# Moving small products next to products of their tile shape in a fused attention and expert kernel

## The chip, the cores and the metric
The kernel runs on one core of a Trainium2 chip. The metric is the device time of one execution in microseconds (us). Before the change it is 894.55 us, the median of three runs (894.02 to 895.84). The engines are TensorE (PE, its weight loads are PEld), VectorE (DVE), ScalarE (ACT), GpSimd (POOL) and SyncE (SP), which issues most DMAs.

## What is computed
The input x has 16 batches of 512 rows of 256 values. Cut to what matters:

```python
xn = layernorm(x)
q = (xn @ Wq.T + bq) * 0.25              # 16 heads of 16
k, v = split(xn @ Wkv.T + bkv)           # one k and one v of 16, shared by all heads
p = softmax(q @ k.T)                     # (16 * 512) x 512 for each batch
attn = (p @ v)(heads side by side) @ Wo.T + bo
g = argmax(xn @ w_gate)                  # one of 6 experts for each row
tok = A[e] @ B[e]; s = softmax(xn @ tok[g].T / 16)
delta = ((s[1:] @ val[g][1:]) + xn) @ wd.T + wd_b, times scale
out = x + attn + xn + log(exp(delta) or eps)
```

## The kernel before, in words
**Tiles.** The attention of one batch is cut into 64 tiles, 1024 in all, numbered t. For tile t TensorE makes two products. The first (line 358, tile shape 64 rows by 128 columns of the array, as only 48 rows are used) gives 128 x 512 scores in a bank of PSUM, of which VectorE takes the row maxima (line 850, into M). The second belongs to tile u = t - 44 (line 363, same shape, 50 rows: two of them bring in the maxima) and gives the scores less their maxima, transposed, in another bank; ScalarE takes the exponential of it into P (line 658). P is a ring of 12 tiles. The two products of a tile use different halves of the array's rows. Here the pair of products is called a tile, and tiles that TensorE does one after another with nothing between them a run.

**P times V.** For every four tiles, 4v to 4v + 3 of the exponentials, TensorE multiplies P with V and a column of ones (line 376, eight instructions, tile shape 128 x 32), and adds over four such steps in the bank pO. The step waits until 4v + 4 exponentials are counted (semaphore e). v lags by LV = 12 quarters: the step of quarter k = v + 12 needs the exponentials made for t = 4k - 4 to 4k - 1.

**Other products of a batch.** Around the tiles stand, once in a batch: Q (q0, q1, line 446) and U with K (uk, line 435), both 128 x 128; V with the gate's logits (vg, line 457, 24 small products of tile shape 128 x 32); the turn (transpose) of that result (vt, line 464, f32, 128 x 128); the expert scores (s, line 471), the turn of their probabilities (p, line 479, four f32 turns), the product a (line 486), d0 to d3 (lines 499 and 501) and the output products o0 to o3 (line 518). Twice in a batch the maxima M are turned (mt, line 507): POOL writes M/2^15 in two f16 pieces into M2, 64 columns wide (lines 983 to 987), TensorE turns it (128 x 64) and ScalarE copies it to MT.

**Due times.** The order of the work is written out by hand. A table SLOT gives for each step of a batch a due time in ticks; one tick is one tile, 64 ticks a batch. FIRST, SECOND, LAST_BUT_ONE and LAST hold other values for those batches. `slots()` turns them into a table of ticks, and each engine goes through the ticks in order and emits, in the order of the branches in its block, what is due. So each engine's program order is fixed. Tiles t and t + 1 of an even t come as a pair at tick t; P times V comes at ticks 4k + 1; the other products have odd ticks. In a steady batch the order on TensorE is pair, P times V, pair, other product, pair, P times V, and so on. The exponential for t is due on ScalarE at t + 0.5, the maximum on VectorE at t + 0.5. The copies on ScalarE go by due times too: the Q copy (qe1, line 607) at tick 24.6 of a batch, the copy of V's product (vge, line 614) at 19.7, the two copies from the turn of V into VK and G (vte, lines 622 and 623) at 27.6. The gate's five steps on VectorE (lines 811 to 822: maximum, compare, priority, maximum, compare) are all due at tick 29.2, one behind the other.

**Banks.** PSUM has eight banks: a ring of four (R1) for the first products of the tiles and most other products, a ring of three (R2) for the second products, vg, vt, p and mt, and pO. The turn in which a product draws a bank follows the due times; a product waits until the one that had the bank before (four, or three, turns back) is freed, by its reader:

```python
before2(name, key): k = TURN[1][name, key] - N2
"ab": (S("e"), t - LB + 1)    # freed by the exponential
"vt": (S("gt"), b + 1)        # freed by the copy of G
"p":  (S("pte"), b + 1)
```

Both waits of a tile, for its bank of four and its bank of three, stand ahead of both its products.

Of the kernel before, what the change touches and what calls it, by code (L numbers as in the profile page):

```python
# [6 lines left out]
F16 = mybir.dt.float16  # L7
# [33 lines left out]
    "residual": 10.2, "q0": -53, "qe0": -51.4, "qs0": -46.5, "qw0": -44, "uk": -49, "uke": -47.4, "ks": -44.2,  # L41
    "kd": -41.6, "vg": -45, "vge": -44.3, "q1": -41, "qe1": -39.4, "qs1": -38.2, "qw1": -35.6,
    "vt": -37, "vte": -36.4, "gate": -34.8, "mask": -32.6, "mkd": -31.4,
    "qread": -25.8, "utm": -24.9, "s": -21,
    "smax": -20.4, "sexp": -18.8, "ssum": -17.4, "snorm": -16.2, "p": -13, "pte": -12.4, "a": -5, "mm": -4.4,
# [6 lines left out]
    "q0": -57, "qe0": -56, "qs0": -55, "qw0": -54, "uk": -53, "uke": -52, "ks": -51, "kd": -50, "q1": -52, "qe1": -51,  # L52
    "qs1": -50, "vg": -50, "vge": -50.5, "vt": -48, "vte": -47, "gate": -46, "mask": -45, "qw1": -40, "mkd": -39,
    "utm": -30, "s": 9, "smax": 9.6, "sexp": 10.2, "ssum": 10.8, "snorm": 11.4, "p": 17, "pte": 17.6, "a": 21, "mm": 21.6,
# [28 lines left out]
PARTH_LAST = {"lr": 86.2, "or": 86.3, "rec": 88.8, "lw": 89.4, "rb": 92.2, "on": 98.3}  # L83

PE_NAMES = ("ab", "pv", "warm0", "warm1", "rg", "xt0", "xt1", "bs", "bw0", "bw1", "w2", "uk", "q0", "q1", "vg", "vt", "s", "p", "a", "d0", "d1",
            "d2", "d3", "mt", "o0", "o1", "o2", "o3", "sl0", "sl1", "oa0", "oa1", "oa2", "oa3", "ob0", "ob1", "ob2", "ob3")
ACT_NAMES = ("root", "xh0", "xh1", "wh", "wdh", "kd", "alpha", "bwe0", "bwe1", "w2e", "uke", "qe0", "qe1", "vge", "vte", "sexp", "pte", "dexp0",
             "dexp1", "dexp2", "dexp3", "dlog0", "dlog1", "mte", "ex", "ot")
DVE_NAMES = ("rngq", "rng", "two", "scl", "wl", "scd", "stats0", "stats1", "stats2", "stats3", "aggr", "refine", "xl0", "xl1",
             "qs0", "gate", "smax", "ssum", "mm", "mx", "rec", "fo0", "fo1", "fo2",  # L90
             "fo3", "nl00", "nl01", "nl02", "nl03", "nl10", "nl11", "nl12", "nl13")
# [5 lines left out]
def slots():  # L97


    at = {}  # L100

    def put(name, slot, key):
        at.setdefault(name, {})[round(100 * slot)] = key

    for b in range(NB):
        special = FIRST if b == 0 else SECOND if b == 1 else LAST_BUT_ONE if b == NB - 2 else LAST if b == NB - 1 else {}
        for name, slot in SLOT.items():
            put(name, 64 * b + special.get(name, slot), b)
    for name, slot in SETUP.items():
        put(name, slot, 0)  # L110
    for name, slot in TAIL.items():
        put(name, 64 * (NB - 1) + slot, NB - 1)
    for n in range(NT + LB):
        put("ab", n - n % 2 + 0.02 * (n % 2) if n < NT else n - n % 4 + 0.02 * (n % 4), n)
        if n >= NT and n % 2:
            put("bd", n - n % 4 + 0.02 * (n % 4), n)
    for n in range(NT):
        put("mx", n + 0.5, n)
        put("ex", n + LB + 0.5, n)
    for v in range(NT // 4):  # L120
        put("pv", 4 * (v + LV + (v + LV >= NT // 4)) + 1, v)
    for g in range(2 * NB):
        for name, slot in HALF.items():
            put(name, 32 * g + 32 + slot, g)
    for g in range(4 * NB):
        for name, slot in QUARTER.items():
            if name == "ot" or g < 4 * NB - 2:
                put(name, 16 * g + slot + 4 * (g >= 4 * NB - 4), g)
    for nh in range(2 * NB - 1):
        for name in PARTH:  # L130
            put(name, 64 * (nh // 2) + (PARTH_LAST[name] if nh == 2 * NB - 2 else PARTH[name][nh % 2]), nh)
    return at
# [14 lines left out]
def build(nc, x, wcat, wqT, woT, wtT, wtb, bq, bkv, bo, wdb, As, Am, scale, out):  # L147
    ctx = ExitStack()
    with ctx:
        def sb(name, shape, dt=F32):  # L150
            return ctx.enter_context(nc.sbuf_tensor(name, shape, dt))
# [6 lines left out]
        def S(name):  # L158
            if name not in sems:
                sems[name] = ctx.enter_context(nc.semaphore("s_" + name))  # L160
            return sems[name]
# [49 lines left out]
        Ms = sb("Ms", [128, 2, H])  # L211
        M2 = sb("M2", [128, 2, 2, H], F16)
        MT = sb("MT", [64, 2, 128], F16)
# [51 lines left out]
        ld = nc.dram_tensor("l_parts", (4, 8 * T), F32, kind="Internal").ap()  # L265

        def bc(ap, n):
            return ap.unsqueeze(len(ap.shape)).to_broadcast(list(ap.shape) + [n])
# [6 lines left out]
        def ticks(*names):  # L275
# [7 lines left out]
            "uk": lambda b: (S("uke"), b + 1), "q0": lambda b: (S("qe0"), b + 1), "q1": lambda b: (S("qe1"), b + 1),  # L283
            "a": lambda b: (S("mm"), b + 1), "rg": lambda b: (S("two"), 2), "bs": lambda b: (S("scl"), 1),
            "o0": lambda b: (S("fo"), 4 * b + 1), "o1": lambda b: (S("fo"), 4 * b + 2),
# [5 lines left out]
        FREED2 = {  # L291
            "ab": lambda t: (S("e"), t - LB + 1), "vg": lambda b: (S("vge"), b + 1),
            "vt": lambda b: (S("gt"), b + 1), "p": lambda b: (S("pte"), b + 1),
# [44 lines left out]
        def _(e):  # L338
            w = Engine(e)
            for n in ticks(*PE_NAMES):  # L340
# [109 lines left out]
                if (b := due("vg", n)) is not None:  # L450
                    w.wait_ge(*before2("vg", b))
                    w.wait_ge(*turned(b))
                    w.wait_ge(S("wcp"), 2)
                    for k, (wp, xp) in enumerate(PIECES):
                        for c in range(2):
                            for i in range(4):
                                mm = e.matmul(bank2("vg", b)[32 * i:32 * i + 32, 0:128], wcP[:, wp, c, V0:V0 + 32],
                                              xT[:, b % 2, i, xp, c, :], start=(k == 0 and c == 0), stop=(k == 2 and c == 1))
                    mm.then_inc(S("vg"))
# [44 lines left out]
                if (g := due("mt", n)) is not None:  # L504
                    w.wait_ge(*before2("mt", g))
                    w.wait_ge(S("m2"), g + 1)
                    e.transpose(bank2("mt", g)[:, :].bitcast(F16)[0:64, 0:128],
                                M2[:, :, :, :].rearrange("p a k h -> p (a k h)"), idh[:, :]).then_inc(S("mt"))

# [32 lines left out]
        def _(e):  # L542
# [6 lines left out]
            for n in ticks(*ACT_NAMES):  # L549
# [60 lines left out]
                if (b := due("vge", n)) is not None:  # L610
                    w.wait_ge(S("vg"), b + 1)
                    w.wait_ge(S("vsc"), 6)
                    w.wait_ge(S("vt"), b)
                    e.activation(VGs[:, :], bank2("vg", b)[:, 0:128], ACT.Identity,
                                 scale=vsc[:, 0:1], bias=vgb[:, 0:1]).then_inc(S("vge"))
# [51 lines left out]
        def _(e):  # L667
# [14 lines left out]
            for n in ticks(*DVE_NAMES):  # L682
# [125 lines left out]

                if (b := due("gate", n)) is not None:
                    w.wait_ge(S("gt"), b + 1)  # L810
                    e.tensor_reduce(gmx[:, :], G[:, :, :], AX, ALU.max).then_inc(S("g0"))
                    w.wait_ge(S("g0"), b + 1)
                    e.tensor_tensor(geq[:, :, :], G[:, :, :], bc(gmx[:, :], NE), ALU.is_equal).then_inc(S("g1"))
                    w.wait_ge(S("g1"), b + 1)
                    w.wait_ge(S("prio"), NE)
                    e.tensor_tensor(gw[:, :, :], geq[:, :, :], prio[:, :].unsqueeze(1).to_broadcast([128, 4, NE]),
                                    ALU.mult).then_inc(S("g2"))
                    w.wait_ge(S("g2"), b + 1)
                    e.tensor_reduce(gm2[:, :], gw[:, :, :], AX, ALU.max).then_inc(S("g3"))
                    w.wait_ge(S("g3"), b + 1)  # L820
                    w.wait_ge(S("mk"), b)
                    e.tensor_tensor(oh[:, :, :], gw[:, :, :], bc(gm2[:, :], NE), ALU.is_equal).then_inc(S("oh"))
# [55 lines left out]
        def _(e):  # L878
            w = Engine(e)
            e.memset(idf[:, :], 0.0).then_inc(S("id"))  # L880
            e.memset(idh[:, :], 0.0).then_inc(S("id"))
            e.memset(mk[:, :, ER:128], 1.0).then_inc(S("mk1"))
            w.wait_ge(S("id"), 2)
            for m in (idf, idh):
# [5 lines left out]
            for n in ticks(*POOL_NAMES):  # L890
# [89 lines left out]
                if (g := due("ms", n)) is not None:  # L980
                    w.wait_ge(S("mx"), 32 * g + 32)
                    w.wait_ge(S("mt"), g)
                    e.tensor_scalar(Ms[:, :, :], M[:, g % 2, :, :], 2.0 ** -15, None, ALU.mult).then_inc(S("ms"))  # L983
                    w.wait_ge(S("ms"), g + 1)
                    e.tensor_copy(M2[:, :, 0, :], Ms[:, :, :]).then_inc(S("m1"))
                    w.wait_ge(S("m1"), g + 1)
                    e.tensor_tensor(M2[:, :, 1, :], Ms[:, :, :], M2[:, :, 0, :], ALU.subtract).then_inc(S("m2"))

# [203 lines left out]
```

## Time and profile before

| what | value |
|---|---|
| median of 3 runs | 894.55 us |
| lowest, highest | 894.02, 895.84 us |
| the profiled execution: its own time | 893.1 us |
| its span, first to last instruction | 891.3 us |
| busy: TensorE, VectorE, ScalarE, POOL | 837.5, 770.9, 687.0, 566.8 us |
| mean granted TensorE clock | 0.973 of full |

All numbers of the trace come from one profiled execution. A time of a matmul is modelled at its end, and matmuls overlap, so the way from the start of one group of products to the start of the next says more than busy time. Idle time of an engine is put down to what ended its last wait. Times in timelines count from the span's start.

### The profile page before, as it was taken

To read this page: it belongs to the slowest core of one execution; us is meant where nothing else is said; L and a number is where in the kernel's file an instruction comes from. 1 tells how busy PE (TensorE), PEld (TensorE's weight loads), DVE (VectorE), ACT (ScalarE), POOL (GpSimd) and SP (SyncE) were. 2 spreads that over 40 slices of the span, in tenths; PEclk is the share of its full clock that TensorE was granted. 3 is DMA by queue.
4 is the path that set the end of the run, shared out by engine and by line. 5 is a ranking of instruction groups with operands and counts; after the bars stand their busy time and mean duration, and the time that the engine had idled before them with its cause. 6 is when DMAs were issued, how large, how long until landed. Compare 5 with 4: busy or idle time off the path is not lost.

```text
span 891.3 us, 18198 instructions
## 1 busy us (share of the span) xinstructions
PE 837.5 (94%) x6038; PEld 276.6 (31%) x6038; DVE 770.9 (86%) x1488; ACT 687.0 (77%) x1386; POOL 566.8 (64%) x754
## 2 busy tenths in 40 slices
PE   6679999999999999999999999999999999999987
PEld 4333223332323332332323233232333333232213
DVE  7688898989989898998989899898989899898926
ACT  2226888888888888888888878888887888888883
POOL 2874677676667767666677766667775766646321
PEclk7688999999999999999999999999999999999989
DMA  4413243634433443534444453443435345241112
GB/s 118 116 41 66 68 101 86 131 86 127 102 97 86 121 107 97 126 93 107 91 109 107 104 120 86 120 98 91 113 97 120 86 119 112 62 105 62 63 52 71
DMA packets 125076, 86.09 MB, mean 97 GB/s; under 512 B 57143, under 2 KB 109112, under 8 KB 124984
## 3 DMA queue, kind: packets, MB, share of 16 engines
q1 hardware_dynamic: 124504, 84.56, 38.5%
q8 instruction: 51, 0.84, 0.4%
q10 hardware_dynamic: 480, 0.36, 0.1%
q14 instruction: 41, 0.34, 0.1%
HBM read 39.30 MB, written 33.54 MB: 82 GB/s over the span
## 4 chain that ended last, share of the span: by engine, by line
PE 76%; DVE 14%; issue 4%; POOL 3%; ACT 2%; DMA 1%; DVEq 0%; POOLq 0%
PE pO L376 24%; PE pA L358 18%; PE pB L363 8%; DVE M L850 8%; PE pA L499 5%; PE pA L446 5%; PE pA L518 4%; PE pA L501 3%; PE pA L435 3%; PE pA L471 2%; PE pA L486 2%; ACT P L658 2%; DVE st L778 1%; PE pB L479 1%; DVE RL L863 1%
## 5 line engine op out<-in xcount | busy, mean ns | idle before, releaser
L850 DVE TENSOR_REDUCE M<-pA 128x1 f32<-128x512 f32 x1024 | 650.0, 681 | 80.3 <-PE pA L358 79.0
L658 ACT ACTIVATE P<-pB 128x512 f32<-128x512 f32 x1002 | 556.5, 605 | 124.8 <-PE pB L363 120.5
L358 PE MATMUL pA<-K,Q 48*128 48x512 f16 x1024 | 320.3, 388 | 27.0 <-DVE M L850 15.0
L363 PE MATMUL pB<-Q,K 50*128 50x512 f16 x1002 | 314.0, 385 | 0.3 <-DVE M L850 0.2
L376 PE MATMUL pO<-P,VK 128*32 128x512 f32 x2048 | 273.9, 607 | 2.0 <-ACT OTr L664 1.1
L358 PEld LDWEIGHTS pA<-K,Q 48*128 48x128 f16 x1024 | 67.8, 94 | 337.7 <-DVE M L850 273.7
L1005 POOL TENSOR_TENSOR Rs<-Rs,Cz 128x512 f32<-128x512 f32 x32 | 40.7, 1272 | 51.1 <-ACT Cz L646 49.0
L376 PEld LDWEIGHTS pO<-P,VK 128*32 128x32 f32 x2048 | 40.6, 108 | 96.7 <-issue 56.8
L998 POOL TENSOR_SCALAR Cz<-Cx 128x512 f32<-128x512 f32 x32 | 62.1, 1941 | 11.5 <-ACT Cx L640 11.5
L363 PEld LDWEIGHTS pB<-Q,K 50*128 50x128 f16 x1002 | 64.1, 94 | 7.4 <-ACT P L658 5.5
L963 POOL CAST Qp<-qf 128x512 f16<-128x512 f32 x31 | 18.9, 610 | 66.4 <-ACT qf L607 66.3
L499 PE MATMUL pA<-wcP,xT 128*128 128x256 f16 x384 | 54.3, 279 | 0.8 <-DVE M L850 0.8
L1013 POOL TENSOR_TENSOR On<-Op,Rb 128x512 f32<-128x512 f32 x31 | 39.8, 1284 | 20.3 <-DMA Rb<-l_parts 19.6
L518 PE MATMUL pA<-woP,OnP 128*128 128x256 f16 x369 | 51.9, 277 | 0.5 <-POOL OnP L1018 0.5
L446 PE MATMUL pA<-xT,wqP 128*128 128x512 f16 x192 | 49.0, 393 | 1.3 <-DVE M L850 0.5
L992 POOL TENSOR_TENSOR En<-Es,sR 128x400 f32<-128x400 f32 x16 | 13.6, 853 | 51.0 <-DVE sR L837 51.0
L640 ACT ACTIVATE Cx<-pA,sc_d 128x256 f32<-128x256 f32 x64 | 30.8, 482 | 15.9 <-PE pA L501 15.9
L499 PEld LDWEIGHTS pA<-wcP,xT 128*128 128x128 f16 x384 | 32.7, 99 | 31.7 <-DVE M L850 17.7
L1000 POOL TENSOR_TENSOR Cx<-Cx,Cz 128x512 f32<-128x512 f32 x32 | 40.7, 1272 | 2.7
L518 PEld LDWEIGHTS pA<-woP,OnP 128*128 128x128 f16 x369 | 31.3, 98 | 32.7 <-DVE M L850 17.9
L983 POOL TENSOR_SCALAR Ms<-M 128x32 f32<-128x32 f32 x32 | 9.7, 302 | 48.5 <-DVE M L850 48.5
L664 ACT COPY OTr<-pO 128x512 f32<-128x512 f32 x64 | 38.0, 594 | 1.8 <-PE pO L376 1.8
(170 smaller groups left out, 897.5 us busy)
## 6 DMA issues: line engine op xcount, KB each, us to landing
o_parts<-OTr SPq DMA_DIRECT2D x62, 256.0 KB, 2.2
X<-in_x SPq DMA_DIRECT2D x16, 512.0 KB, 3.9
q_pieces<-Qp SPq DMA_DIRECT2D x64, 128.0 KB
out<-OUT SPq DMA_DIRECT2D x32, 256.0 KB, 3.4
Op<-o_parts SPq DMA_DIRECT2D x31, 256.0 KB
Rb<-l_parts SPq DMA_DIRECT2D x31, 256.0 KB
Q<-q_pieces SPq DMA_DIRECT2D x30, 256.0 KB, 4.7
Q<-q_pieces SPq DMA_DIRECT2D x34, 128.0 KB, 4.6
```

Source lines behind the costliest of these rows:

```text
L358: e.matmul(bank1("ab", t)[:, :], Q16[r:r + 48, b % 3, h, 128 * s:128 * s + 128], K16[r:r + 48, b % 3, :], start=True, stop=True).then_inc( ...
L363: e.matmul(bankB(t)[:, :], K16[r:r + 50, b % 3, 128 * i:128 * i + 128], Q16[r:r + 50, b % 3, :, 32 * hh:32 * hh + 32], start=True, stop=Tr ...
L376: mm = e.matmul(pO[32 * j:32 * j + 32, :], VK[:, b % 3, i, :], P[:, p % PR, :], start=(i == 0), stop=(i == 3))
L446: mm = e.matmul(bank1(f"q{g}", b)[:, :], wqP[:, wp, c, 128 * g:128 * g + 128], xT[:, b % 2, :, xp, c, :], start=(k == 0 and c == 0), stop= ...
L499: e.matmul(dst, xT[:, b % 2, t, xp, c, :], wcP[:, wp, c, 0:C], start=(k == 0 and c == 0), stop=False)
L518: mm = e.matmul(bankO(t, b), OnP[:, b % 2, part, op, 128 * t:128 * t + 128], woP[:, wp, part, :], start=(part == 0 and k == 0), stop=(part ...
L658: e.activation(P[:, u % PR, :], bankB(u + LB)[:, :], ACT.Exp, scale=alpha).then_inc(S("e"))
L850: e.tensor_reduce(M[:, t // 32 % 2, t % 2, t % 32 // 2:t % 32 // 2 + 1], bank1("ab", t)[:, :], AX, ALU.max, negate=True).then_inc(S("mx"))
L998: e.tensor_scalar(cz, cx, 0.0, F32_EPS, ALU.is_equal, ALU.mult).then_inc(S("c0"))
L1000: e.tensor_tensor(cx, cx, cz, ALU.add).then_inc(S("c1"))
L1005: e.tensor_tensor(Rs[:, b % 5, 2 * k:2 * k + 2, :], Rs[:, b % 5, 2 * k:2 * k + 2, :], Cz[:, 2 * k:2 * k + 2, :], ALU.add).then_inc(S("r2"))
L1013: e.tensor_tensor(On[:, :].rearrange("p (t h) -> p h t", h=H), Op[:, :].rearrange("p (h t) -> p h t", h=H), Rb[:, :].rearrange("p (h t) -> ...
```

## The change
The kernel's tables of due times and the code that reads them change, and four things with them.

- **Runs.** A list STRETCH gives the ticks of a batch at which a run of tiles begins. It holds the even ticks, except that ticks 18 to 23, 26 to 31 and 50 to 55 are each cut into two runs of three. PV_AT moves the P times V step of quarters 5, 7 and 13 from ticks 21, 29 and 53 to 20.5, 28.5 and 52.5, between the two runs of three.
- **Small products.** V's product vg moves from tick 19 to 17.1, directly behind the P times V step of tick 17, and from the ring of three to the ring of four. The turn of V moves from tick 27 to 23.1, directly behind q1, and the turn of the probabilities from tick 51 to 55.1, directly behind o3. Their copies on ScalarE move: vge from 19.7 to 17.7, vte from 27.6 to 25.8, pte from 51.6 to 55.7. In a steady batch the runs and products of like tile shape that follow one another form 58 groups instead of 66.
- **M's turn.** M2 becomes 128 columns wide, its upper 64 filled with zeros once by POOL; the turn is 128 x 128 and stands where it stood, behind d1 and o2.
- **Gate.** The five steps on VectorE are due at 27.8, 28.8, 29.8, 30.8 and 31.3, with maxima between them; the mask on POOL moves from 31.4 to 31.8.

```diff
-    "kd": -41.6, "vg": -45, "vge": -44.3, "q1": -41, "qe1": -39.4, "qs1": -38.2, "qw1": -35.6,
-    "vt": -37, "vte": -36.4, "gate": -34.8, "mask": -32.6, "mkd": -31.4,
+    "kd": -41.6, "vg": -46.9, "vge": -46.3, "q1": -41, "qe1": -39.4, "qs1": -38.2, "qw1": -35.6,
+    "vt": -40.9, "vte": -38.2, "gate0": -36.2, "gate1": -35.2, "gate2": -34.2, "gate3": -33.2, "gate4": -32.7,
+    "mask": -32.2, "mkd": -31.4,
...
-    "smax": -20.4, "sexp": -18.8, "ssum": -17.4, "snorm": -16.2, "p": -13, "pte": -12.4, "a": -5, "mm": -4.4,
+    "smax": -20.4, "sexp": -18.8, "ssum": -17.4, "snorm": -16.2, "p": -8.9, "pte": -8.3, "a": -5, "mm": -4.4,
...
+STRETCH = (0, 2, 4, 6, 8, 10, 12, 14, 16, 18, 21, 24, 26, 29, 32, 34, 36, 38, 40, 42, 44, 46, 48, 50, 53, 56, 58, 60, 62)
+PV_AT = {5: 0.5, 7: 0.5, 13: 0.5}
...
+    def stretch(n):
+        k = n % 64
+        first = max(m for m in STRETCH if m <= k) if n < NT else k - k % 4
+        return n - k + first + 0.02 * (k - first)
+
     for n in range(NT + LB):
-        put("ab", n - n % 2 + 0.02 * (n % 2) if n < NT else n - n % 4 + 0.02 * (n % 4), n)
+        put("ab", stretch(n), n)
...
     for v in range(NT // 4):
-        put("pv", 4 * (v + LV + (v + LV >= NT // 4)) + 1, v)
+        k = v + LV + (v + LV >= NT // 4)
+        put("pv", 4 * k + (PV_AT.get(k % 16, 1) if k < NT // 4 else 1), v)
...
-        M2 = sb("M2", [128, 2, 2, H], F16)
+        M2 = sb("M2", [128, 128], F16)
...
+        M2v = M2[:, 0:64].rearrange("p (a k h) -> p a k h", a=2, k=2)
...
-                    w.wait_ge(*before2("vg", b))
+                    w.wait_ge(*before1("vg", b))
...
-                    e.transpose(bank2("mt", g)[:, :].bitcast(F16)[0:64, 0:128],
-                                M2[:, :, :, :].rearrange("p a k h -> p (a k h)"), idh[:, :]).then_inc(S("mt"))
+                    w.wait_ge(S("mz"), 1)
+                    e.transpose(bank2("mt", g)[:, :].bitcast(F16)[:, 0:128], M2[:, :], idh[:, :]).then_inc(S("mt"))
...
+            e.memset(M2[:, 64:128], 0.0).then_inc(S("mz"))
```

In FREED1 and FREED2 the entry of vg moves with it, and `due("gate", n)` is split into five branches of one step each, with the same waits.

## Rows read from the trace of the kernel before

**Rows 1.** The page: span of the profiled execution.
```profile
span 891.3 us, 18198 instructions
```

**Rows 2.** Busy time in one stretch: us, PE, PEld, DVE, ACT, POOL, clock, DMA, GB/s.
```profile
394.20:445.70 51.50, 50.26 (x374) 16.10 (x375) 46.42 (x89) 42.71 (x87) 35.62 (x47) 1.00 0.43 105
```

**Rows 3.** Timeline of TensorE (start, us, engine, line, operation, count): V's product.
```profile
358.31 0.52 PE L457 MATMUL pB<-xT,wcP 128*32 128x128 f16 x24
```

**Rows 4.** Timeline of TensorE, next batch: pair 18, V's product, q1, pair 24.
```profile
409.02 0.39 PE L358 MATMUL pA<-K,Q 48*128 48x512 f16 x1
...
409.75 0.52 PE L457 MATMUL pB<-xT,wcP 128*32 128x128 f16 x24
...
412.68 1.47 PE L446 MATMUL pA<-xT,wqP 128*128 128x512 f16 x6
414.08 0.39 PE L358 MATMUL pA<-K,Q 48*128 48x512 f16 x1
```

**Rows 5.** Timeline of TensorE, same batch, ticks 51 to 56: from the turn of probabilities on.
```profile
435.52 0.65 PE L479 MATMUL pB<-idf,En 128*100 128x128 f32 x4
436.19 0.37 PE L358 MATMUL pA<-K,Q 48*128 48x512 f16 x1
...
437.00 1.06 PE L376 MATMUL pO<-P,VK 128*32 128x512 f32 x8
437.99 0.39 PE L358 MATMUL pA<-K,Q 48*128 48x512 f16 x1
...
438.53 0.83 PE L518 MATMUL pA<-woP,OnP 128*128 128x256 f16 x6
439.30 0.39 PE L358 MATMUL pA<-K,Q 48*128 48x512 f16 x1
```

**Rows 6.** Timeline, last batch: a run of four tiles and the step behind it.
```profile
813.13 0.39 PE L358 MATMUL pA<-K,Q 48*128 48x512 f16 x1
...
813.36 0.59 PE L358 MATMUL pA<-K,Q 48*128 48x512 f16 x2
...
813.59 1.08 ACT L658 ACTIVATE P<-pB 128x512 f32<-128x512 f32 x2 [0.45 <-PE pB L363]
...
814.73 0.64 PE L376 MATMUL pO<-P,VK 128*32 128x512 f32 x4
```

**Rows 7.** Timeline of TensorE, first batch: the three small products between first products.
```profile
46.40 0.64 PE L479 MATMUL pB<-idf,En 128*100 128x128 f32 x4
46.97 0.43 PE L358 MATMUL pA<-K,Q 48*128 48x512 f16 x2
47.33 0.52 PE L457 MATMUL pB<-xT,wcP 128*32 128x128 f16 x24
47.78 0.45 PE L358 MATMUL pA<-K,Q 48*128 48x512 f16 x2
...
54.20 0.33 PE L464 MATMUL pB<-idf,VGs 128*128 128x128 f32 x1
54.46 0.44 PE L358 MATMUL pA<-K,Q 48*128 48x512 f16 x2
```

**Rows 8.** Timeline of ScalarE behind pair 24: Q copy, exponentials, copy of G.
```profile
415.03 0.77 ACT L607 ACTIVATE qf<-pA,bq_s,scl 128x512 f32<-128x512 f32 x1
415.69 1.57 ACT L658 ACTIVATE P<-pB 128x512 f32<-128x512 f32 x3
...
417.21 0.23 ACT L623 COPY G<-pB 128x24 f32<-128x24 f32 x1
```

**Rows 9.** Timeline, ticks 27 to 33: VectorE around the gate's steps, then P times V.
```profile
416.83 0.42 DVE L778 BATCH_NORM_STATS2 st<-X 128x6 f32<-128x256 f32 x1
...
418.62 0.17 DVE L811 TENSOR_REDUCE gmx<-G 128x4 f32<-128x24 f32 x1
...
419.59 1.88 DVE L850 TENSOR_REDUCE M<-pA 128x1 f32<-128x512 f32 x3
...
421.25 1.07 PE L376 MATMUL pO<-P,VK 128*32 128x512 f32 x8
```

More of the change, by code:

```diff
@@ L52 @@
     "q0": -57, "qe0": -56, "qs0": -55, "qw0": -54, "uk": -53, "uke": -52, "ks": -51, "kd": -50, "q1": -52, "qe1": -51,
-    "qs1": -50, "vg": -50, "vge": -50.5, "vt": -48, "vte": -47, "gate": -46, "mask": -45, "qw1": -40, "mkd": -39,
+    "qs1": -50, "vg": -50, "vge": -50.5, "vt": -48, "vte": -47, "gate0": -46, "gate1": -45.9, "gate2": -45.8, "gate3": -45.7, "gate4": -45.6, "mask": -45, "qw1": -40, "mkd": -39,
     "utm": -30, "s": 9, "smax": 9.6, "sexp": 10.2, "ssum": 10.8, "snorm": 11.4, "p": 17, "pte": 17.6, "a": 21, "mm": 21.6,
@@ L89 @@
 DVE_NAMES = ("rngq", "rng", "two", "scl", "wl", "scd", "stats0", "stats1", "stats2", "stats3", "aggr", "refine", "xl0", "xl1",
-             "qs0", "gate", "smax", "ssum", "mm", "mx", "rec", "fo0", "fo1", "fo2",
+             "qs0", "gate0", "gate1", "gate2", "gate3", "gate4", "smax", "ssum", "mm", "mx", "rec", "fo0", "fo1", "fo2",
              "fo3", "nl00", "nl01", "nl02", "nl03", "nl10", "nl11", "nl12", "nl13")
@@ L283, in build @@
             "uk": lambda b: (S("uke"), b + 1), "q0": lambda b: (S("qe0"), b + 1), "q1": lambda b: (S("qe1"), b + 1),
-            "a": lambda b: (S("mm"), b + 1), "rg": lambda b: (S("two"), 2), "bs": lambda b: (S("scl"), 1),
+            "a": lambda b: (S("mm"), b + 1), "vg": lambda b: (S("vge"), b + 1), "rg": lambda b: (S("two"), 2), "bs": lambda b: (S("scl"), 1),
             "o0": lambda b: (S("fo"), 4 * b + 1), "o1": lambda b: (S("fo"), 4 * b + 2),
@@ L291, in build @@
         FREED2 = {
-            "ab": lambda t: (S("e"), t - LB + 1), "vg": lambda b: (S("vge"), b + 1),
+            "ab": lambda t: (S("e"), t - LB + 1),
             "vt": lambda b: (S("gt"), b + 1), "p": lambda b: (S("pte"), b + 1),
@@ L456, in _ @@
                             for i in range(4):
-                                mm = e.matmul(bank2("vg", b)[32 * i:32 * i + 32, 0:128], wcP[:, wp, c, V0:V0 + 32],
+                                mm = e.matmul(bank1("vg", b)[32 * i:32 * i + 32, 0:128], wcP[:, wp, c, V0:V0 + 32],
                                               xT[:, b % 2, i, xp, c, :], start=(k == 0 and c == 0), stop=(k == 2 and c == 1))
@@ L613, in _ @@
                     w.wait_ge(S("vt"), b)
-                    e.activation(VGs[:, :], bank2("vg", b)[:, 0:128], ACT.Identity,
+                    e.activation(VGs[:, :], bank1("vg", b)[:, 0:128], ACT.Identity,
                                  scale=vsc[:, 0:1], bias=vgb[:, 0:1]).then_inc(S("vge"))
@@ L807, in _ @@
                     e.tensor_tensor(Qp[:, 0, 1, :], qf[:, 0, :], Qp[:, 0, 0, :], ALU.subtract).then_inc(S("ql0"))
-                if (b := due("gate", n)) is not None:
+                if (b := due("gate0", n)) is not None:
                     w.wait_ge(S("gt"), b + 1)
                     e.tensor_reduce(gmx[:, :], G[:, :, :], AX, ALU.max).then_inc(S("g0"))
+                if (b := due("gate1", n)) is not None:
                     w.wait_ge(S("g0"), b + 1)
                     e.tensor_tensor(geq[:, :, :], G[:, :, :], bc(gmx[:, :], NE), ALU.is_equal).then_inc(S("g1"))
+                if (b := due("gate2", n)) is not None:
                     w.wait_ge(S("g1"), b + 1)
@@ L817, in _ @@
                                     ALU.mult).then_inc(S("g2"))
+                if (b := due("gate3", n)) is not None:
                     w.wait_ge(S("g2"), b + 1)
                     e.tensor_reduce(gm2[:, :], gw[:, :, :], AX, ALU.max).then_inc(S("g3"))
+                if (b := due("gate4", n)) is not None:
                     w.wait_ge(S("g3"), b + 1)
@@ L984, in _ @@
                     w.wait_ge(S("ms"), g + 1)
-                    e.tensor_copy(M2[:, :, 0, :], Ms[:, :, :]).then_inc(S("m1"))
+                    e.tensor_copy(M2v[:, :, 0, :], Ms[:, :, :]).then_inc(S("m1"))
                     w.wait_ge(S("m1"), g + 1)
-                    e.tensor_tensor(M2[:, :, 1, :], Ms[:, :, :], M2[:, :, 0, :], ALU.subtract).then_inc(S("m2"))
+                    e.tensor_tensor(M2v[:, :, 1, :], Ms[:, :, :], M2v[:, :, 0, :], ALU.subtract).then_inc(S("m2"))
                 if (b := due("snorm", n)) is not None:
```

## The prediction
> **What bounds the kernel now.** I read the page first, then the timeline of one batch on each engine, then the places where two groups of products stand further apart than elsewhere. The span is 891.3 us [rows 1], the execution's own time 893.1, the median of the three runs 894.55, 0.2% above it; I work in differences, made against the profiled execution and added to the median. In a stretch of 51.5 us TensorE is busy 50.26, VectorE 46.42 and ScalarE 42.71, at the full granted clock [rows 2]. The V product of one batch starts at 358.31 [rows 3], that of the next at 409.75 [rows 4]: 51.44 us a batch, and batches 3 to 13 all show that period to 0.02. So TensorE's program order is the kernel's clock: what lengthens the way from one of its groups to the next is paid in each of the batches 1 to 14.
>
> The costs of groups, from start to start of the next: a pair of tiles (two score products, two for the exponential) 0.54, a P times V step 1.00, an O product 0.77 [rows 5], a Q product of six streams of 512 columns 1.40 [rows 4]. The tiles of one run follow each other 0.23 apart [rows 6], so a pair costs 0.08 beyond its streams; the Q product, its six streams spread over 1.47 with about 0.39 for the last, 0.10. That is my price for one change of tile shape: 0.09. The Trainium skill ("TensorEngine Tiling (Array Packing)", Key Properties) says that changing the tiling mode drains TensorE, and "TensorE: Matmul & The Clock Gate", Part 2, puts a drain at about 128 cycles, 0.053 us at 2.4 GHz. By that estimate the shape changes saved below would bring some 0.04 less each, and the time would be about 3 us above my forecast; the rows decide for 0.09.
>
> Beside the shapes there are waits. The pair before the V product takes 0.73 [rows 4] and the pair behind the turn of the probabilities 0.81 instead of 0.54, that turn itself 0.67 [rows 5], while in the first batch, where the ring of three serves no tiles yet, it takes 0.57, the V product 0.45 and the turn of V 0.26 [rows 7]. All three draw a bank from the ring of three, which ScalarE frees.
>
> **The change, part by part.** S18 is the start of the run that begins with tile 18 of a batch, and so on. A run of three costs 0.54 + 0.23 = 0.77.
>
> *Runs of three.* The P times V step of quarter k needs the exponentials of tiles 4k-4 to 4k-1. Today a pair and mostly a product more stand between tile 4k-1 and the step. After the change the steps at 20.5, 28.5 and 52.5 stand directly behind the runs 18-20, 26-28 and 50-52 and need tiles 19, 27 and 51, the second of their run. The last batch shows today what that is: a run of four from 813.13, whose second tile the step behind it needs. ScalarE starts 0.46 later, ends the second exponential at 813.59 + 1.08 = 814.67, and the step starts at 814.73, 1.60 after the run [rows 6]. So each of the three steps starts 1.60 and not 0.77 after its run: a **new wait of 0.83**. Queued behind it on TensorE are the next run and all that follows, and on ScalarE and VectorE those who wait for that run. The Trainium skill speaks against this change too ("TensorE: Matmul & The Clock Gate", Part 3: matmuls keep strictly to their order, only weight loads are pulled ahead); the trace agrees, as no product passes the waiting step before 814.73.
>
> *Ticks 17 to 23.* Before: the step 1.00, then 409.02 to 412.68, 3.66: 4.66 [rows 4]. After: the step less one change of shape, 0.91; V's product 0.45; 1.60; the step 1.00; a run 0.77: 4.73, plus what ScalarE still has ahead of exponential 18 (the copies of U and K and of V). That is nothing at least, and 0.77 at most, the longest such copy, that of Q [rows 8]; most of it fits into the 1.36 ahead of the run, so I take 0.1. Sum 4.83: **+0.17**.
>
> *Ticks 23 to 33, the turn of V.* Before: 412.68 to 421.25, 8.57 [rows 4, 9]. After: the Q product 1.40 - 0.09 and the turn 0.26, so S24 = 1.57. Here the ring matters. The turn now draws its bank ahead of tiles 24, 25 and 26, so tile 26 gets the very bank that the turn holds until ScalarE has copied G, and that copy keeps its place behind exponential 25. From ScalarE's rows, against the pair at 414.08 [rows 4]: the Q copy comes at +0.95, exponential 25 at +1.61; the third of the exponentials from 415.69 starts at 415.69 + 1.57 - 0.60 = 416.66 and G 0.55 later, for 0.23 [rows 8]. G is free at 1.61 + 0.55 + 0.23 = 2.39, and TensorE restarts 0.06 later as in [rows 6]. So S26 = S24 + 2.45 and not + 1.54: a **second new wait, 0.9**. Then S26 is 4.02, the step 5.62, S29 6.62, the O product 7.39, S32 8.16, tile 33 ready at 8.39.
> VectorE meanwhile: maximum 26 starts 0.42 after S26. The way from 416.83 (statistics) to 419.59 (maximum 29) is 2.76 and holds five gate steps in 0.97, 0.19 each; three maxima in 1.88 are 0.60 apart, the last 0.68 [rows 9]. With three of the five steps left behind the start of maximum 29, maximum 30 ends 0.60 + 2.76 - 0.58 + 0.60 + 0.19 + 0.68 = 4.25 after the start of maximum 26: at 4.02 + 0.42 + 4.25 = 8.69. Tile 33 starts at 8.75, P times V 0.31 later at 9.06: **+0.49**. Spreading the gate's steps adds no work and takes none away; it frees ticks 31 and 32 of their wait, but leaves two steps, 0.39, behind maximum 30. What of these reaches TensorE at ticks 35 and 37 lies between 0 and 0.39; I take **+0.25**, since some slack eats the rest.
>
> *Turn of M.* At ticks 3 and 35 it takes the shape of the product ahead: one change less, twice: **-0.18**. Its weight load of 128 columns for 64 lies beside a running stream; uncovered it would cost under 0.1. The new fill of M2 is one POOL memset in the setup, ahead of a stretch in which TensorE only warms up: 0; if that cover went, once 0.2.
>
> *Ticks 50 to 56, the turn of the probabilities.* Before: 0.54 + 0.67 + 0.81 + 0.99 + 0.54 + 0.77 = 4.32 [rows 5]. After: 1.60 + 1.00 + 0.77 + (0.77 - 0.09) + 0.57 = 4.62: **+0.30**. Its copy on ScalarE is needed only at tick 59, three groups on: 0, or one such copy, 0.6, late without them.
>
> Sum for a batch: 0.17 + 0.49 + 0.25 - 0.18 + 0.30 = **+1.03**, times 14 = 14.4. Batch 0 has no exponentials at those ticks and waits for VectorE there: 0, give or take 0.5. In the last batch runs of four, 1.60 already, become runs of three and five: about +0.3. Together +14.7: 907.8 for such an execution as was profiled, **909.2** for the median.
>
> **Rivals.**
> *The turn's bank is free in time (chance 0.12).* If G is copied before tile 26 asks, the 0.9 goes, though exponential 26 still queues behind it to about S24 + 2.4 where it could start at 2.0: some 0.6 is won, +0.4 a batch, and with +0.3 for the last 894.55 + 5.9 = 900.5. Against it: the order of ScalarE's queue is written out, and the Q copy stands in it ahead.
> *Unlike products keep their change (0.10).* If the five changes saved around the turns and V's product bring nothing, because the streams differ in type or bank, it is 0.45 a batch worse: 909.2 + 6.3 = 915.5. The merged runs are safe, by [rows 6].
> *Faster (0.09).* The three steps behind the runs of three find their exponentials done. Then three times 0.83 goes, 1.03 - 2.49 = -1.46 a batch: 894.55 - 20.4 + 0.3 = 874.5. It decides from the point where a step starts less than 1.26 after its run, 0.34 sooner than 1.60. For it: the change removes waits of the size seen at 0.73 and 0.81 [rows 4, 5], and VectorE has 5 us a batch to give [rows 2]. Against it: the run of four in [rows 6] is the same order of work, and it waits.
> The forecast has 0.62; 0.07 is left for gains and losses that meet near zero. That the change does not do what it says is no case: tables of due times set the order, and nothing else does.
>
> **The numbers.** Likeliest 909.2. Downwards the range takes in the free bank, upwards most of the kept changes and the copies ahead of exponential 18: 899 to 915. A measurement of this kernel can tell 0.2%, 1.8 us. Slower by more has 0.62 + 0.12 + 0.10, less 0.01 for their near ends: 0.83; faster 0.09; the same 0.08.
>
> **What would show it.** A batch period of 52.4 to 52.6. The steps behind the runs of three 1.6 after them, TensorE's idle time put down to the exponentials; tile 26 about 0.9 later than now behind its P times V step, put down to the copy of G; V's product at 0.45 to 0.5, the turn of V under 0.3, no pairs of 0.73 and 0.81. The prediction is wrong if those steps come 0.8 after their runs, if tile 26 does not wait, or if the period is 51.4 or less.

## The result, and the profile after

The changed kernel takes 921.36 us (median of 4, 919.58 to 921.99) against 894.28 us beside it: a ratio of 1.0298, 95% interval 1.0276 to 1.032. The forecast was 909.2 with a range of 899 to 915: the right direction, just over half of the size, and outside the range.

Which view: the page of the changed kernel, its span, the busy time of four engines, and the start of the chain that ended last by engine.

```profile
span 917.8 us, 18139 instructions
PE 824.1 (90%) x6038; PEld 279.5 (30%) x6038; DVE 770.5 (84%) x1488; ACT 682.6 (74%) x1386; POOL 566.8 (62%) x755
PE 71%; ACT 14%; issue 5%; DVE 3%; POOL 3%; DMA 3%; SPq 1%; DVEq 0%; ACTq 0%; POOLq 0%
```

TensorE is busy 13 us less and the span is 26.5 us longer: this is waiting. ScalarE now has 14% of the chain, where it had 2% and VectorE 14% before. The busy time in one steady batch answers to [rows 2]:

```profile
459.80:512.50 52.70, 48.81 (x372) 16.27 (x371) 46.35 (x88) 42.33 (x87) 35.59 (x47) 1.00 0.41 102
```

From [rows 3] to [rows 4] a batch took 51.44; now it takes 52.68. TensorE is busy 48.81 of it instead of 50.26, so its work is about 1.4 shorter, and 2.7 of new idle time took its place. Next, the timeline of TensorE from V's product to the P times V step of tick 28.5 in one batch, the stretch that [rows 4] opens (start, us, engine, line, operation, count, idle time before and what ended it):

```profile
474.39 0.52 PE L469 MATMUL pA<-xT,wcP 128*32 128x128 f16 x24
474.84 0.39 PE L370 MATMUL pA<-K,Q 48*128 48x512 f16 x1
...
476.56 1.06 PE L388 MATMUL pO<-P,VK 128*32 128x512 f32 x8 [0.84 <-ACT P L670]
477.55 0.39 PE L370 MATMUL pA<-K,Q 48*128 48x512 f16 x1
...
478.31 1.47 PE L458 MATMUL pA<-xT,wqP 128*128 128x512 f16 x6
479.62 0.27 PE L476 MATMUL pB<-idf,VGs 128*128 128x128 f32 x1
479.82 0.39 PE L370 MATMUL pA<-K,Q 48*128 48x512 f16 x1
...
480.36 1.07 PE L388 MATMUL pO<-P,VK 128*32 128x512 f32 x8
482.36 0.37 PE L370 MATMUL pA<-K,Q 48*128 48x512 f16 x1 [0.93 <-ACT G L635]
...
483.94 1.06 PE L388 MATMUL pO<-P,VK 128*32 128x512 f32 x8 [0.75 <-ACT P L670]
```

All that was forecast for these ticks can be read here. V's product takes 0.45 (474.39 to 474.84), the turn of V 0.20. The step behind run 18 to 20 starts 1.72 after it and that behind run 26 to 28 1.58 after it, both put down to the exponential. Tile 26 starts 2.00 after its P times V step, put down to the copy of G, which ends 0.15 before it on ScalarE:

```profile
482.00 0.21 ACT L635 COPY G<-pB 128x24 f32<-128x24 f32 x1
```

An exponential also ends the wait behind the run of tick 50 (554.25 to 555.85 is 1.60), and behind it the turn of the probabilities stands next to the O product, which [rows 5] showed apart:

```profile
554.25 0.39 PE L370 MATMUL pA<-K,Q 48*128 48x512 f16 x1
...
555.85 1.07 PE L388 MATMUL pO<-P,VK 128*32 128x512 f32 x8 [0.77 <-ACT P L670]
556.84 0.39 PE L370 MATMUL pA<-K,Q 48*128 48x512 f16 x1
...
557.60 0.83 PE L530 MATMUL pA<-woP,OnP 128*128 128x256 f16 x6
558.27 0.60 PE L491 MATMUL pB<-idf,En 128*100 128x128 f32 x4
558.80 0.39 PE L370 MATMUL pA<-K,Q 48*128 48x512 f16 x1
```

What was not forecast comes at tick 32. The pair takes 1.38. Before it took 0.92, and its tiles waited for VectorE (P times V at 421.25 in [rows 9]):

```profile
420.33 0.39 PE L358 MATMUL pA<-K,Q 48*128 48x512 f16 x1 [0.23 <-DVE M L850]
```

Timelines of TensorE and of ScalarE there now:

```profile
486.46 0.39 PE L370 MATMUL pA<-K,Q 48*128 48x512 f16 x1
...
486.95 0.37 PE L370 MATMUL pA<-K,Q 48*128 48x512 f16 x1
...
487.83 1.07 PE L388 MATMUL pO<-P,VK 128*32 128x512 f32 x8 [0.49 <-ACT P L670]
```

```profile
485.40 0.60 ACT L670 ACTIVATE P<-pB 128x512 f32<-128x512 f32 x1 [1.02 <-PE pB L375]
485.89 0.20 ACT L565 ACTIVATE lv<-ve 128x4 f32<-128x4 f32 x1
486.12 0.20 ACT L567 ACTIVATE y<-lv 128x4 f32<-128x4 f32 x1
486.23 0.58 ACT L670 ACTIVATE P<-pB 128x512 f32<-128x512 f32 x1
486.71 0.58 ACT L676 COPY OTr<-pO 128x512 f32<-128x512 f32 x1
487.17 1.59 ACT L670 ACTIVATE P<-pB 128x512 f32<-128x512 f32 x3
```

Tile 33 starts at 486.95, about where VectorE's chain puts it, but P times V could only start at 487.83: the exponential of tile 31 starts at 487.17, behind two steps of the layer norm's root and the copy of the sums. ScalarE stood idle for 1.02 until run 29 to 31 (from 484.94 on) gave it work. From there one chain leads to P times V, from start to start: 0.46 to the exponential of tile 29, 0.49 for it, 0.34 for the root, 0.48 for the exponential of tile 30, 0.46 for the copy of the sums, 0.66 for the exponential of tile 31 and the restart, 2.89 in all.

Of the 26.5 us, fourteen times 1.24 are 17.4. The rest lies in single batches: batch 1 costs 3.5 more than that, and in two others, 4 and 14, TensorE's clock falls behind the two waits of tick 25 to 28 and costs 1.8. Busy time by stretch in batch 4 and, in the last row, in batch 1, the granted clock third from the end:

```profile
265.00:271.00 6.00, 5.07 (x37) 1.50 (x31) 4.76 (x11) 3.73 (x9) 1.16 (x3) 1.00 0.36 108
271.00:274.00 3.00, 2.25 (x13) 0.18 (x10) 2.65 (x10) 1.57 (x3) 0.91 (x2) 0.71 0.33 92
274.00:277.00 3.00, 2.88 (x20) 0.97 (x16) 2.33 (x7) 2.29 (x7) 1.06 (x5) 0.72 0.26 88
277.00:283.00 6.00, 5.89 (x45) 2.29 (x47) 5.67 (x10) 4.51 (x11) 5.69 (x14) 1.00 0.52 131
115.00:122.00 7.00, 6.59 (x29) 1.04 (x29) 3.84 (x7) 3.48 (x8) 6.62 (x15) 0.50 0.26 72
```

The means of 0.71 and 0.72 hold some 3.4 us at half clock, the 1.2 GHz level. Before that stretch TensorE stood still for 0.93 and then 0.75, with a run in between. In batch 1 the clock is at half from 111.8 to 122.1, behind the same two waits. That batch takes 55.24, 2.56 more than a steady one, and all of this arises in these ten us; the other 0.9 is that batch 1 of the kernel before took 50.52, less than its steady 51.44. In batches 3, 10 and 11 the O product of tick 7 waits 0.3 to 0.7 for POOL (1.4 together), the first batch takes 0.8 more and what follows the start of the last one 1.4 more. Sum: 26.3 of the 26.5.

### The profile page after: what moved, and what is told of

Same layout as the page of the kernel before. It is cut to its first block, busy times and chain, and to the rows that moved or that the text cites. A ratio compares the mean times of both kernels' runs of the same rounds, so it can differ in the third digit from the quotient of the medians.

```text
span 917.8 us, 18139 instructions
## 1 busy us (share of the span) xinstructions
PE 824.1 (90%) x6038; PEld 279.5 (30%) x6038; DVE 770.5 (84%) x1488; ACT 682.6 (74%) x1386; POOL 566.8 (62%) x755
## 4 chain that ended last, share of the span: by engine, by line
PE 71%; ACT 14%; issue 5%; DVE 3%; POOL 3%; DMA 3%; SPq 1%; DVEq 0%; ACTq 0%; POOLq 0%
PE pO L388 23%; PE pA L370 16%; ACT P L670 10%; PE pB L375 7%; PE pA L458 5%; PE pA L511 5%; PE pA L530 4%; PE pA L513 3%; PE pA L447 2%; PE pA L483 2%; PE pA L498 1%; ACT UK L611 1%; DVE M L870 1%; ACT qf L619 1%; DMA Rb<-l_parts 1%
## 5 line engine op out<-in xcount | busy, mean ns | idle before, releaser
L370 PE MATMUL pA<-K,Q 48*128 48x512 f16 x1024 | 311.3, 391 | 25.2 <-ACT G L635 13.1
L388 PE MATMUL pO<-P,VK 128*32 128x512 f32 x2048 | 277.6, 615 | 44.0 <-ACT P L670 42.9
L375 PE MATMUL pB<-Q,K 50*128 50x512 f16 x1002 | 304.6, 388 | 0.3 <-ACT P L670 0.2
L513 PE MATMUL pA<-W,MmT 98*128 98x256 f32 x128 | 38.8, 385 | 0.0
```

Source lines behind the costliest of these rows:

```text
L370: e.matmul(bank1("ab", t)[:, :], Q16[r:r + 48, b % 3, h, 128 * s:128 * s + 128], K16[r:r + 48, b % 3, :], start=True, stop=True).then_inc( ...
L375: e.matmul(bankB(t)[:, :], K16[r:r + 50, b % 3, 128 * i:128 * i + 128], Q16[r:r + 50, b % 3, :, 32 * hh:32 * hh + 32], start=True, stop=Tr ...
L388: mm = e.matmul(pO[32 * j:32 * j + 32, :], VK[:, b % 3, i, :], P[:, p % PR, :], start=(i == 0), stop=(i == 3))
L513: e.matmul(dst, MmT[0:ER + 2, 128 * t:128 * t + 128], W2[0:ER + 2, :], start=False, stop=True).then_inc(S("d"))
```

## The experiments

Times by tick are medians of a trace's steady batches, from the start of a group on TensorE to the start of the next.

**Runs of four.** Pairs and P times V at 4k + 1 again; where the small products have left, two pairs meet.

```diff
-STRETCH = (0, 2, 4, 6, 8, 10, 12, 14, 16, 18, 21, 24, 26, 29, 32, 34, 36, 38, 40, 42, 44, 46, 48, 50, 53, 56, 58, 60, 62)
-PV_AT = {5: 0.5, 7: 0.5, 13: 0.5}
+STRETCH = tuple(range(0, 64, 2))
+PV_AT = {}
```

> The changed kernel with runs of pairs again and P times V at ticks 4k + 1; as the small products stay where the change put them, pairs 18 and 20, 26 and 28, 50 and 52 now meet and make runs of four ahead of the step. Theory (a P times V step waits for the exponential of the second tile of the run ahead, 1.60 us after its start, however many tiles the run has): each such region saves one tile's 0.12 on the first run (1.60 for four tiles instead of 1.60 to 1.72 for three) and 0.22 on the second (0.54 for two instead of 0.76 for three), some 0.3 three times, so a batch period of 51.7 to 52.0 instead of 52.68 and about 909 us. Tile 26 still waits for the copy of G, 2.0 from P times V to it. Rival (the wait comes from runs longer than two, so the longer the run, the worse): the steps come 2 us or more after the runs of four and the period stays at 52.7 or above, 921 us or more. Rival (shapes): same number of shape changes, so no difference, 921.

Measured: 897.3 us, ratio to the kernel before 1.0021 (1.0005 to 1.0036); period 51.58. The steps come 1.72, 1.58 and 1.60 after runs of four, the same as after runs of three:

```profile
515.71 0.39 PE L370 MATMUL pA<-K,Q 48*128 48x512 f16 x1
...
517.42 1.07 PE L388 MATMUL pO<-P,VK 128*32 128x512 f32 x8
518.42 0.39 PE L370 MATMUL pA<-K,Q 48*128 48x512 f16 x1
```

So the delay depends on the tile needed and not on the number of tiles, and the fourth tile is free. Three tiles ahead of the step and three behind cost 0.22 a region more than four and two, 0.66 a batch; the pair of tick 32 falls from 1.38 to 0.85, and 0.08 comes back at ticks 34 and 36. The two rivals are out: neither longer waits nor an equal time. The period is 0.1 below the range given, since tick 32 had not been foreseen in it, and the time is lower than 14 times 1.10 makes it (24 us less than the changed kernel, not 15): the clock's falls in batches 1, 4 and 14 went too, and so did the waits of tick 7 in two of the three batches.

**The copy of G early.**

```diff
-    "vt": -40.9, "vte": -38.2,
+    "vt": -40.9, "vte": -39.7,
```

> The changed kernel with one due time moved: the two copies out of the turn of V (VK and G) on ScalarE at tick 24.3, ahead of exponential 24 and of the Q copy, instead of 25.8. Theory (tile 26 waits for the bank that the turn of V holds until G is copied): P times V at tick 25 to tile 26 falls from 2.00 to 1.00; exponential 26 then still queues behind the Q copy, so the step behind run 26 to 28 comes 1.9 after the run instead of 1.58, net 0.5 to 0.7 a batch, period 52.0 to 52.2, 911 to 914 us, and the dips of TensorE's clock at ticks 28 to 31 of single batches go, 2 to 5 us more. Rival (tile 26 waits for ScalarE's exponentials or for VectorE in any case): still 1.8 or more from that P times V to tile 26, no change in time, 921.

Measured: 906.65 us, ratio 1.0123 (1.0099 to 1.0148); period 51.81.

```profile
526.52 1.07 PE L388 MATMUL pO<-P,VK 128*32 128x512 f32 x8
527.52 0.39 PE L370 MATMUL pA<-K,Q 48*128 48x512 f16 x1
...
529.23 0.64 PE L388 MATMUL pO<-P,VK 128*32 128x512 f32 x4 [0.49 <-ACT P L670]
```

The 2.00 is 1.00, and the step comes 1.70 after run 26 to 28 instead of 1.58: 0.87 a batch, more than the 0.5 to 0.7 expected, as the step behind the run came 0.2 sooner than the 1.9 given; the time is below the 911 to 914. From batch 1 to the last tiles the clock stays at 1.00. Batch 0 takes 60.45 instead of 56.92, with more time at half clock; why is not shown. The wait for the turn's bank is shown.

**Runs shifted by one.** The same three and three tiles, but the step needs the first tile of its run.

```diff
-... 14, 16, 18, 21, 24, 26, 29, 32, ..., 48, 50, 53, 56, 58, 60, 62)
-PV_AT = {5: 0.5, 7: 0.5, 13: 0.5}
+... 14, 16, 19, 22, 24, 27, 30, 32, ..., 48, 51, 54, 56, 58, 60, 62)
+PV_AT = {4: 2.5, 5: 1.5, 6: 2.5, 7: 1.5, 12: 2.5, 13: 1.5}
-    "vg": -46.9, "vge": -46.3
+    "vg": -45.4, "vge": -45.3
```

> The changed kernel with the runs of three moved by a tile: 16 to 18, 19 to 21 and then the pair 22, 23 (and 24-26, 27-29, 30-31; 48-50, 51-53, 54-55), each P times V step behind its run as before, V's product still behind the step of quarter 4. The step of quarters 5, 7 and 13 now needs the first tile of the run ahead, not the second. Theory: it starts 1.11 after the run (0.46 to the exponential, 0.60 for it, 0.05) instead of 1.60; the step of quarters 4, 6 and 12 needs tiles of earlier runs and comes 0.77 after its run. 0.4 to 0.6 saved three times, except where G's copy rules; period 51.3 to 51.9, 901 to 911 us. Rival (the wait is that of a bank in the ring of three, not of the data of P): the same number of tiles stands between the same products, so the steps still come 1.6 after their runs, period 52.5 or more, 919 us or more.

Measured: 922.8 us, ratio 1.0311 (1.029 to 1.0331), with a period of 52.64 where the clock stays up: no gain, so both the 901 to 911 us and the period of 51.3 to 51.9 were missed. Where ScalarE has nothing else, at tick 51, the mechanism holds to 0.01:

```profile
558.13 0.39 PE L370 MATMUL pA<-K,Q 48*128 48x512 f16 x1
...
558.59 1.09 ACT L670 ACTIVATE P<-pB 128x512 f32<-128x512 f32 x2 [0.55 <-PE pB L375]
...
559.24 0.64 PE L388 MATMUL pO<-P,VK 128*32 128x512 f32 x4 [0.28 <-ACT P L670]
```

1.11 after the run, against 1.60 for the second tile: the data of P decide, and the rival (a bank) is out at this place. At ticks 19 and 27 the step comes 1.36 after its run instead of 1.72 and 1.58. Two other things gave the gain back. The runs of three now come before the steps of quarters 4, 6 and 12 too, and draw the third bank while ScalarE copies: tile 26 stands in run 24 to 26 and waits there for G, so that run takes 2.86, and run 48 to 50 takes 1.45. And the clock falls to half for 3.4 us in batch 1 and in eight of the batches from 3 on, each time from tick 26 or 27 on; such a batch takes 53.87, 1.2 more. The wait ahead of one fall, and the stretch behind it:

```profile
320.02 0.39 PE L370 MATMUL pA<-K,Q 48*128 48x512 f16 x1
...
322.56 0.37 PE L370 MATMUL pA<-K,Q 48*128 48x512 f16 x1 [1.93 <-ACT G L635]
```

```profile
323.00:327.00 4.00, 4.00 (x22) 0.51 (x19) 2.79 (x11) 2.33 (x6) 0.89 (x2) 0.57 0.38 112
```

**Gate and M alone,** in the kernel before: the gate's five steps between maxima, M2 over 128 columns, nothing else.

```diff
-"gate": -34.8, "mask": -32.6,
+"gate0": -36.2, "gate1": -35.2, "gate2": -34.2, "gate3": -33.2, "gate4": -32.7, "mask": -32.2,
-        M2 = sb("M2", [128, 2, 2, H], F16)
+        M2 = sb("M2", [128, 128], F16)
```

> The kernel before with two parts of the change alone: the gate's five steps between maxima (ticks 27.8 to 31.3) and M2 over 128 columns. The two act at different ticks and are told apart in the trace. Theory: M's turn saves 0.12 at ticks 3 and 35 (measured in the changed kernel), the gate's steps save nothing of VectorE's work but move the wait from ticks 31 and 32 (1.06 and 0.92 before) to ticks 32 and 36; together between -0.1 and -0.4 a batch, 888 to 893 us against 894. Rival (the gate's steps between maxima are themselves a cost, through a fixed price of each change of instruction on VectorE): ticks 31 to 37 grow by 0.3 or more, period above 51.5, 895 to 899 us.

Measured: 887.41 us, ratio 0.9916 (0.9895 to 0.9938); period 50.90, 0.54 less. The O product of tick 31 falls from 1.06 to 0.76 and the pair behind it from 0.92 to 0.78, of which the pair of tick 36 gives back 0.11: 0.33 for the gate, more than expected. M's turn saves 0.12 at tick 3 and 0.12 at tick 35. P times V of tick 33 now waits 0.18 for an exponential, so that here too ScalarE, and no longer VectorE, ends the pair of tick 32:

```profile
519.34 0.83 PE L520 MATMUL pA<-woP,OnP 128*128 128x256 f16 x6
520.10 0.39 PE L360 MATMUL pA<-K,Q 48*128 48x512 f16 x1
...
520.88 0.64 PE L378 MATMUL pO<-P,VK 128*32 128x512 f32 x4 [0.18 <-ACT P L660]
```

Two of the change's parts are gains, 0.8% together, and with the rest of it the kernel takes 34 us more.

**The ring of four.** If the small products had been dear for their banks and not for their shape, it is enough to change the ring, at the old ticks. Alone, and with gate and M:

```diff
+            "vg": lambda b: (S("vge"), b + 1), "vt": lambda b: (S("gt"), b + 1), "p": lambda b: (S("pte"), b + 1),   # FREED1
-            "vg": ..., "vt": ..., "p": ...                                                                       # FREED2
-before2("vg", b), bank2("vg", b)      # and vt, p
+before1("vg", b), bank1("vg", b)
```

> The kernel before with one thing changed: V's product, the turn of V and the turn of the probabilities draw their banks from the ring of four, at their old ticks 19, 27 and 51. Theory (what these three cost before was the ring of three, and not their tile shape): pairs 18, 20, 26, 28 and 52 fall from 0.73 to 0.81 to 0.54, V's product to 0.45, the turn of V to 0.26 to 0.30, that of the probabilities to 0.57: 0.59, 0.78 and 0.36 less, some 1.7 a batch, of which VectorE, behind at ticks 28 to 36, gives back 0.2 to 0.8; period 49.8 to 50.5, 872 to 882 us. Rival (their cost was the change of shape, which stays): period 51.3 to 51.5, 893 to 896 us.

> The same with the two parts of the change that gained alone, the gate's steps between maxima and M2 over 128 columns. Theory: the parts add, as they act on different waits, except that VectorE at ticks 26 to 36 now rules: period 49.2 to 50.0 (50.90 with gate and M alone, less 0.9 to 1.7), 862 to 874 us; below both kernels. Rival (VectorE, 46.4 busy of a batch, is already the bound there): period 50.5 or more, 882 us or more.

Measured: 883.6 us, ratio 0.9866 (0.9845 to 0.9888), period 50.68; and 873.06 us, ratio 0.9755 (0.9733 to 0.9777), period 49.94. Timeline of the first, from the turn of V and at the O product of tick 31:

```profile
513.45 0.33 PE L464 MATMUL pA<-idf,VGs 128*128 128x128 f32 x1
513.71 0.39 PE L358 MATMUL pA<-K,Q 48*128 48x512 f16 x1
...
514.24 0.39 PE L358 MATMUL pA<-K,Q 48*128 48x512 f16 x1
...
516.12 0.83 PE L518 MATMUL pA<-woP,OnP 128*128 128x256 f16 x6
517.60 0.39 PE L358 MATMUL pA<-K,Q 48*128 48x512 f16 x1 [0.65 <-DVE M L850]
```

Pairs 18 and 26 fall from 0.73 to 0.56, V's product to 0.45, the turn of V to 0.26, that of the probabilities and the pair behind it to 0.58 and 0.55. The rival is out, but the period misses its 49.8 to 50.5 and the time its 872 to 882 us: less is saved than the 1.7 expected, 1.25, as pair 20 only falls to 0.69, and pair 28 rises from 0.81 to 0.88. The O product of tick 31 rises from 1.06 to 1.48, within what VectorE was expected to give back, because its next pair waits for the maxima behind the gate's five steps in a row. With the steps spread it is 0.76 again, so the two parts add to more than their sum: 50.90 and 50.68 apart, 49.94 together. In it TensorE is busy 49.63 of 50.00 us and VectorE 45.94:

```profile
501.10:551.10 50.00, 49.63 (x375) 15.86 (x371) 45.94 (x89) 42.28 (x87) 36.09 (x48) 1.00 0.44 108
```

This version beats both kernels.

**All due times of the change repaired.** Runs of four, the copy of G early, the turn of the probabilities back at tick 51.

```diff
+STRETCH = tuple(range(0, 64, 2)); PV_AT = {}
+"vte": -39.7, "p": -13, "pte": -12.4
```

> The changed kernel with all three repairs of due times: runs of pairs and P times V at 4k + 1, the copies of VK and G at tick 24.3, and the turn of the probabilities and its copy back at ticks 51 and 51.6. Only V's product behind P times V and the turn of V behind q1 stay, beside gate and M. Theory (additive by ticks, from the changed kernel's 52.68: -1.10 for the runs as measured, -0.87 for the copy of G as measured, -0.02 for the probabilities): period 50.65 to 50.75, 883 to 887 us, that is 0.2 a batch better than gate and M alone. Rival (the repairs free the same time twice, since the copy of G and the runs act on the same stretch of ticks 24 to 33): period 51.0 to 51.4, 888 to 895 us.

Measured: 884.99 us, ratio 0.9891 (0.9866 to 0.9917), period 50.75, as expected. With V's product behind P times V and the turn of V behind q1 kept, the change is worth 0.15 a batch beyond gate and M (50.90): that is what two of its three moves brought, with the waits behind the runs of four still in.

**The root later.** In the changed kernel, and in the version with the ring of four.

```diff
-    "root": -98.2, "refine": -97.2,
+    "root": -96.1, "refine": -96,
```

> The changed kernel with the two small steps of the layer norm's root on ScalarE (logarithm and exponential of 128 x 4) due at tick 31.9 instead of 29.8, behind the exponential of tile 31, and the refinement on POOL behind them. Open: why the pair at tick 32 takes 1.38 in the changed kernel. Theory (P times V of tick 33 waits for the exponential of tile 31, which on ScalarE follows the run 29 to 31, the root and the copy of the sums): without the root in between, tile 31's exponential ends about 0.34 sooner, the pair takes 1.0 to 1.1, period 52.3 to 52.4, 914 to 917 us beside 921. Rival (VectorE's maxima of tiles 29 and 30 with the gate's steps between them set it, as the prediction had it): 1.38 stays, period 52.68.

> The ring of four with gate and M (873 us) and the root later as in the run before. There the pair at tick 32 takes 0.93 and the exponential of tile 31 is done before P times V asks for it by the trace, so VectorE sets it. Theory: no gain, 0.93 stays, period 49.9 to 50.0, 872 to 875 us. Rival (the copies on ScalarE hold up tiles there too): 0.6 to 0.8, period 49.7, 869 to 871 us.

Measured: the pair of tick 32 takes 1.06 in the first, 0.32 less, P times V still put down to the exponential:

```profile
535.48 0.39 PE L370 MATMUL pA<-K,Q 48*128 48x512 f16 x1
...
535.82 0.39 PE L370 MATMUL pA<-K,Q 48*128 48x512 f16 x1
...
536.53 0.64 PE L388 MATMUL pO<-P,VK 128*32 128x512 f32 x4 [0.32 <-ACT P L670]
```

So ScalarE's two small steps ahead of exponential 31 make 0.32 of that wait; the rest stays. The O product of tick 35 takes back 0.21, as M's turn behind it waits for an exponential, and the pair behind that turn takes 0.11 less: the period is 52.46, above the 52.3 to 52.4 expected. In five batches the clock falls from tick 28 on and costs about 0.9 each, so the time is hardly lower, 919.62 us (ratio 1.0274, 1.0238 to 1.031), above the 914 to 917 expected. In the second, where VectorE sets that pair, it stays at 0.93 and the time at 873.92 us (ratio 0.9771, 0.9753 to 0.9788): no gain, as expected, and the period 50.07, 0.13 more than without the edit.

## Why the prediction was wrong

By the prediction's own steps, a batch, forecast and measured:

| step | forecast | measured |
|---|---|---|
| ticks 17 to 23 | +0.17 | +0.15 |
| ticks 23 to 33, turn of V | +0.49 | +0.96 |
| ticks 33 to 37, gate's rest, with M's turn | +0.16 | -0.01 |
| M's turn at tick 3 | -0.09 | -0.12 |
| ticks 50 to 56 | +0.30 | +0.24 |
| sum (period) | +1.03 | +1.22 (1.24) |

Right were the two waits that the prediction named, each in its place, with its size and its releaser: 1.58 to 1.72 for the steps behind runs of three, and the bank of the turn of V with a restart at S24 + 2.54 (2.45 forecast). Both were confirmed by taking the cause away: 1.11 with the first tile needed, 1.00 with the copy of G early. The price of a shape change was right too: 0.12 at the step before V's product, 0.09 at q1, 0.12 for M. The first two rivals, that G's bank is free and that unlike products keep their change, are out, and so is the faster one.

Two steps failed. The first is "tile 33 starts at 8.75, P times V 0.31 later at 9.06": that step of the chain follows VectorE alone. P times V at tick 33 also needs exponential 31, and ScalarE has the root and the copy of the sums ahead of it; with that it was 9.53, that is 0.47 a batch or 6.6 us too little. The later runs show the place: moving the root alone takes 0.32 off. It is in part luck that the sum for a batch is only 0.2 off: the gate's leftover and ticks 50 to 56 were put too high. The second is "times 14 = 14.4", with 0 give or take 0.5 for the first batch and +0.3 for the last: it takes TensorE's clock and the edges as they were. Of the 26.5 us 17.4 are periods, where 14.4 were forecast; 9 are outside the periods, where 0.3 was. So of the 12 us by which the forecast is short, 3 are periods, which alone would have left it inside its range, and 9 are this second step. Some 4.4 of the 9 are falls of the clock: 1.8 in batches 4 and 14, and 2.6 in batch 1, with its ten us at half clock. Why the clock fell in these three batches and not in the others, which have the same waits, stays open. What the first batch (0.8), the end and the O products of tick 7 in three batches add (1.4 each) was not tried apart.

The gate's leftover, +0.25 between 0 and 0.39, was put too high: the pair of tick 36 takes 0.65 instead of 0.54, 0.11 more, in the changed kernel and with gate and M alone. That spreading the steps "frees ticks 31 and 32 of their wait" was right: alone it takes 0.44 off there and saves 0.33 in all. In the changed kernel only the 0.30 of the O product is left of it, since the pair of tick 32 then waits for ScalarE.

## What to carry to other kernels

When groups are merged, list for every waiting step which instruction it needs and where that one now stands, on each engine that feeds it: a consumer that stood one product behind its producer pays the whole latency when the product between them goes. Before moving an operation for its tile shape, look at which ring its buffer comes from: here changing the ring, at the old places, brought 1.3% alone and 2.4% with gate and M (which bring 0.8% by themselves), while the moves brought 0.15 us a batch at best. No run tried the moves together with the ring of four for all three products. And measure the parts alone, for a gain can be hidden behind a loss in the same stretch.

## What the runs showed of the hardware

TensorE's granted clock fell from 2.4 to 1.2 GHz for 3.4 us without any long pause ahead: in batch 4 of the changed kernel behind 0.93 and 0.75 us of idle time with a run of three between them; in batch 1 it stayed low for 10.2 us behind the same two waits, and in most other batches of the same trace the same waits left it at 1.00. The runs shifted by one had it in eight steady batches, behind a wait of 1.93, with the root later in five, the copy of G early and the runs of four in none of batches 1 to 14. "TensorE: Matmul & The Clock Gate" of the Trainium skill ("Why this matters for your kernels") warns of idle gaps between bursts of matmuls that are longer than any of these; here none ahead of a fall in a steady batch reached 2 us, and what decides between batches with the same waits no run took apart. Each fall of 3.4 us in a steady batch cost 0.7 to 1.2 us.

TensorE kept its order strictly over waits of up to 1 us (476.56, 482.36, 487.83 above). It starts again 0.06 us behind an exponential (487.17 and 0.60 to 487.83, with the 0.60 of a single one) and 0.15 us behind the copy of G (482.00 and 0.21 to 482.36).
